# Latent attention and LoRA feed-forward on one core: low parts of the feed-forward's operands made earlier, folds moved to GpSimd, residual loaded in two transfers

## Chip, cores and metric

The kernel runs on one core of a Trainium2 chip. The metric is the device time of one execution in microseconds. The median of three runs before the change is 580.56 us. TensorE multiplies matrices into banks of PSUM; VectorE, ScalarE and GpSimd work element by element; SyncE (SP) issues the transfers. The engines run side by side and wait for each other's semaphores.

## The reference

x has 2 x 512 tokens of 512 features. Two sublayers with a layer norm before and after each:

```
x = x + layernorm(attention(layernorm(x)))     # 32 heads, latent (low-rank) queries, keys and values
x = x + layernorm(ffn(layernorm(x)))

def _qlora_linear(x, wq, A, B):                # the weight is wq repeated 4 times along its input
    return x @ tile(wq, (1, 4)).T + (x @ A.T @ B.T) * 0.5
gate = silu(_qlora_linear(x, w1q, a1, b1))     # 512 -> 1376, wq 1376 x 128, rank 2
up   = _qlora_linear(x, w3q, a3, b3)
ffn  = _qlora_linear(gate * up, w2q, a2, b2)   # 1376 -> 512, wq 512 x 344
```

Because the weight repeats 4 times, x can be folded: the four quarters of its features are added (512 to 128) and multiplied once with wq.

## The kernel before

All products are kept near float32 accuracy by splitting: an operand is written as a high part (rounded, written by ScalarE in the type fp32r) and a low part (the rest, a subtraction by VectorE or GpSimd), and `three` issues three matmuls: high x high, high x low, low x high. Much of the work of the other engines is the making of these parts.

The order of every engine is written out by hand. After the attention (until about 419 us) come three stages.

*Projection.* Eight tiles of 128 tokens. TensorE runs `project(t, hh)`: 24 matmuls for each half hh of the heads, 48 a tile. VectorE and ScalarE go through steps t = 0 to 8 beside it. In step t VectorE takes, for tile u = t-1: statistics of the product, `split_output(t, 1)` (low part of the second half of tile t, 128x1024), the first layer norm's factors, the last two of tile u-1's four `lora_dots`, the residual sum `x1 += z` (the first waits for the load of x1), statistics of the sum, `second_scale`, `split_output(t+1, 0)`, `fold_sum(u)` (a reduction of xn2 from 512 to 128 columns), the first two `lora_dots(u)` (a multiplication of xn2 with a row of a1 or a3, summed, one for each of the 4 ranks) and `lora_lo`. ScalarE makes z (layer norm of the product), xn2 (normalised sum) and the high parts. TensorE turns the folds and dots of tile t-2 in the middle of `project(t, 1)` (`turn_y`). Between the steps stand pieces for the feed-forward: in step 5 VectorE makes 3 of 12 gate/up low parts (`split_gate`), in step 6 the low part of bs_s (the LoRA-up factors, 128x1376), in step 7 the low part of the first 512 tokens' activations (xf_lo). Tile 7's second norm, fold and dots are done inside the feed-forward.

*Feed-forward.* Two halves of 512 tokens with 12 groups G each (G = 0 to 23, 128 or 88 hidden units). A group is six matmuls (gate and up), and after every second group `low_rank` adds the LoRA parts of two groups. ScalarE applies Silu, VectorE multiplies (`gu`), GpSimd adds four groups' gu into fs. Two banks' worth of lead is all TensorE has: `gate_or_up(1, G)` waits for the gu of G-3, `gate_or_up(0, G)` for its Silu; groups below 12 also wait for their `split_gate`, group 12 for the second xf_lo. `lora_down` multiplies gu with a2. In the first half VectorE makes 9 `split_gate`, tile 7's fold and dots, the b2 pair (b2 and b2_s, LoRA-down bias factors), the second xf_lo, and at group 11 wd_lo (128x1536).

*Tail.* Eight tiles of the down projection, layer norm and output.

SP issues, behind the last attention transfers: x1 (2 MB), then, once all `split_weights` are done, a13 (1 MB), w13 (1.4 MB), bs (0.7 MB); after the whole projection a2 and b2; after tile 7's dots wd.

Of the kernel before, what the change touches and what calls it, by code (L numbers as in the profile page):

```python
# [26 lines left out]
P = 128  # L27
# [58 lines left out]
def build(nc, x_d, wa_d, lnw_d, cst_d, kcs_d, sq_d, sv_d, w13_d, bs_d, a13_d, a2_d, w2_d, b2_d, out_d):  # L86
# [87 lines left out]
    w13 = pro.take("w13", [P, 2, HID])  # L174
    pr2 = Map(nc, late, late + 4 * 6 * D)
# [6 lines left out]
    ffn = Map(nc, start + 4 * P + 32 + CST_BYTES, late)  # L182
    w13_hi = ffn.take("w13_hi", [P, 2, HID], F32R)
    w13_lo = ffn.take("w13_lo", [P, 2, HID], F32R)
    bs_s = ffn.take("bs_s", [P, HID], F32R)
    xf_hi = ffn.take("xf_hi", [P, TOK], F32R)
    xf_lo = ffn.take("xf_lo", [P, TOK], F32R)
    b2 = ffn.take("b2", [P, D])
    a2 = ffn.take("a2", [P, RT, FOLD, 32])
    b2_s = ffn.take("b2_s", [P, D], F32R)  # L190
# [36 lines left out]
    def sems(phase, words):  # L227
# [13 lines left out]
    c = sems("projection", """xn2_made wv_in0 wv_in1 wv_in2 wv_copied wv_hi_made wv_split o_hi_made o_split o_used x1_in w13_in bs_in a13_in  # L241
        dve_step std1_made z_made std2_made fold_made dots_raw dots_made lt_zero y_turned xt2_moved lp_hi_made lp_split""")
# [8 lines left out]
    with block:  # L251

        @block.sync
        def _(sp):
# [82 lines left out]
            sp.dma_start(x1[:, :, :], xb.rearrange("t p d -> p t d")).then_inc(c.x1_in, 16)  # L337
            sp.wait_ge(c.wv_split, PAIRS)
            sp.dma_start(a13[:, :, :], a13_d).then_inc(c.a13_in, 16)
            sp.dma_start(w13[:, :, :], w13_d).then_inc(c.w13_in, 16)  # L340
            sp.dma_start(bs[:, :], bs_d).then_inc(c.bs_in, 16)

            sp.wait_ge(c.o_used, 2 * TB)
            sp.dma_start(a2[:, :, :, :], a2_d).then_inc(g.a2_in, 16)
            sp.dma_start(b2[:, :], b2_d).then_inc(g.b2_in, 16)
# [13 lines left out]
        def _(pool):  # L359
# [66 lines left out]

            for hf in range(2):
                for r in range(RT):
                    n = RROWS[r]
                    for k in range(1, FOLD):  # L430
                        pool.wait_ge(g.gu_made, 12 * hf + 4 * r + k + 1)
                        if (hf, r, k) != (0, 0, 1):
# [3 lines left out]
                                                gu[0:n, at(k), :], ALU.add).then_inc(g.fold_added, 1)  # L436


        @block.scalar
        def _(act):  # L440
# [80 lines left out]
            def normalise_sum(u):  # L521

                act.wait_ge(c.dve_step, 9 * u + 9)
                if u:
                    act.wait_ge(c.dots_made, u)
                nc.scalar.activation(xn2[:, :], x1[:, u, :], ACT.Identity, scale=st2[:, 11:12],
                                     bias=st2[:, 12:13]).then_inc(c.xn2_made, 1)
# [122 lines left out]
            for t in range(TB + 1):  # L650
# [21 lines left out]
                if t in (3, 4):  # L672
                    nc.scalar.activation(w13_hi[:, t - 3, :], w13[:, t - 3, :], ACT.Copy).then_inc(g.w_hi_made, 1)
                if t == 5:
                    act.wait_ge(c.o_split, 10)
                    act.wait_ge(c.bs_in, 16)
                    nc.scalar.activation(bs_s[:, :], bs[:, :], ACT.Copy, scale=cst[:, 3 * SEQ + 5:3 * SEQ + 6]).then_inc(g.bs_hi_made, 1)
# [13 lines left out]
            for hf in range(2):  # L691
                for n in range(12):
# [6 lines left out]
                    if G == 1:  # L699
                        second_deviation(TB - 1)  # L700
                        normalise_sum(TB - 1)
# [8 lines left out]
                    if G == 8:  # L710
# [8 lines left out]
                    if G == 7:  # L719
                        act.wait_ge(g.b2_in, 16)  # L720
                        nc.scalar.activation(b2_s[:, :], b2[:, :], ACT.Copy).then_inc(g.b2_hi_made, 1)
# [13 lines left out]
        def _(dve):  # L735
# [248 lines left out]
            for t in range(TB + 1):  # L984
# [5 lines left out]
                if 0 <= t - 1 < TB:  # L990
# [5 lines left out]
                    if u:  # L996
                        lora_dots(u - 1, (2, 3))
                    dve.wait_ge(c.z_made, u + 1)
                    if u == 0:
                        dve.wait_ge(c.x1_in, 16)  # L1000
                    step(nc.vector.tensor_tensor(x1[:, u, :], x1[:, u, :], zb[:, :], ALU.add), c.dve_step)
                    statistics(st2, x1[:, u, :], c.dve_step)
                    if t < TB:
# [3 lines left out]
                        fold_sum(u)  # L1007
                        lora_dots(u, (0, 1))
                if 2 <= t < TB:
                    lora_lo(t - 2)  # L1010
                if t == 5:
                    for n in range(3):
                        split_gate(n)
                if t == 6:
# [3 lines left out]
                if t == 7:  # L1018
# [18 lines left out]
            for hf in range(2):  # L1037
                for n in range(12):
# [8 lines left out]
                    if G + 3 < 12:  # L1047
                        split_gate(G + 3)
                    if G == 1:
                        second_scale(TB - 1)  # L1050
                    if G == 2:
                        fold_sum(TB - 1)
                    if G in (2, 3, 4, 5):
                        lora_dots(TB - 1, (G - 2,))
# [7 lines left out]
                    if G == 11:  # L1062
# [467 lines left out]
```

## Time and profile before

| | before |
|---|---|
| runs, us | 580.56, 580.23, 584.92 (median 580.56) |
| profiled execution | 581.56 us, of which the span of its instructions 579.7 |
| TensorE clock granted | 0.996 |
| TensorE, VectorE, ScalarE, GpSimd busy | 96%, 77%, 68%, 34% |

TensorE's busy share is near 100% almost everywhere; in the 40 slices of the span it falls a little in the feed-forward and more in the tail. Times in the trace count from the span's start. Matmuls overlap: one of 512 columns is listed with 0.39 us, but the next starts 0.23 us later. VectorE's instructions overlap by about 0.08 us in the same way.

### The profile page before, as it was taken

How to read it: one execution, taken by the hardware profiler on the slowest of the kernel's cores; microseconds unless marked ns; L12 is line 12 of the kernel's file. 1: busy time of each engine (PE TensorE's matmuls, PEld its weight loads, DVE VectorE, ACT ScalarE, POOL GpSimd, SP SyncE). 2: the span in 40 equal slices, each digit the busy share in tenths (PEclk: the TensorE clock that was granted, in tenths of full speed). 3: DMA queues.
4: the chain of work that ended last, by engine and by line, in shares of the span. 5: the costliest groups of instructions: out<-in, count | busy, mean ns of one | idle time of the engine just before them, and what ended most of it. 6: DMA issues, size and time to landing. Idle time of an engine off the chain costs nothing. (4 is left out here: it accounts for less than half of the span.)

```text
span 579.7 us, 10859 instructions
## 1 busy us (share of the span) xinstructions
PE 557.4 (96%) x3274; PEld 424.5 (73%) x3274; DVE 447.1 (77%) x1206; ACT 396.1 (68%) x1173; POOL 196.4 (34%) x204
## 2 busy tenths in 40 slices
PE   7999999999999999999999999999999999988996
PEld 6676778777787787787878878876678888645565
DVE  5877787787677777877887787888859889877467
ACT  4566778887888787878878888878733553444344
POOL 3125354344443543444344444441000000036520
PEclk8999999999999999999999999999999999999999
DMA  9911223212312222131111101006580000101003
GB/s 325 354 56 51 79 61 118 79 52 87 121 52 79 86 94 79 52 112 53 52 35 55 50 21 47 20 26 201 174 331 1 1 0 1 32 1 54 1 19 128
DMA packets 22009, 46.93 MB, mean 81 GB/s; under 512 B 2880, under 2 KB 5696, under 8 KB 21696
## 3 DMA queue, kind: packets, MB, share of 16 engines
q1 hardware_dynamic: 21952, 46.23, 23.8%
q8 instruction: 28, 0.46, 0.3%
q14 instruction: 29, 0.24, 0.1%
HBM read 39.80 MB, written 6.42 MB: 80 GB/s over the span
## 5 line engine op out<-in xcount | busy, mean ns | idle before, releaser
L766 DVE CUSTOM_DVE_ANT_0 ss<-bank,cst 128x128 f32<-128x128 f32 (+3 forms) x256 | 125.0, 489 | 72.0 <-PE bank L1130 40.9
L485 ACT ACTIVATE pt<-bank 128x128 f32<-128x128 f32 (+3 forms) x256 | 110.1, 430 | 63.2 <-PE bank L1198 62.9
L477 ACT ACTIVATE pr<-ss,small 128x128 f32<-128x128 f32 (+3 forms) x256 | 143.2, 559 | 5.8 <-DVE small L766 4.3
L373 POOL TENSOR_TENSOR qrot<-qrot,qswp 64x512 f32<-64x512 f32 x64 | 82.1, 1283 | 116.2 <-DVE qrot L758 113.7
L1198 PE MATMUL bank<-ident,pr 128*128 128x128 f32 x640 | 113.7, 275 | 1.6 <-ACT pr L477 1.5
L1198 PEld LDWEIGHTS bank<-ident,pr 128*128 128x128 f32 x640 | 78.4, 141 | 23.6 <-ACT pr L477 6.0
L380 POOL TENSOR_TENSOR qt_lo<-qrot,qt_hi 128x384 fp32r<-128x384 f32 x64 | 64.6, 1009 | 72.4 <-ACT qt_hi L467 71.3
L1128 PE MATMUL bank<-kt_hi,qt_hi 128*128 128x256 f32 (+2 forms) x192 | 80.7, 421 | 0.3 <-DVE small L766 0.3
L1210 PE MATMUL bank<-pt,kvn 128*64 128x256 f32 (+3 forms) x512 | 75.2, 434 | 0.7 <-ACT pt L485 0.7
L1210 PEld LDWEIGHTS bank<-pt,kvn 128*64 128x64 f32 x512 | 38.8, 137 | 41.0 <-issue 28.1
L1130 PE MATMUL bank<-kt_hi,qt_lo 128*128 128x256 f32 (+2 forms) x192 | 65.1, 339 | 0.0
L1129 PE MATMUL bank<-kt_lo,qt_hi 128*128 128x256 f32 (+2 forms) x192 | 64.7, 337 | 0.0
L1128 PE MATMUL bank<-wv,o_s 128*128 128x512 f32 x128 | 51.5, 402 | 1.3 <-DVE o_s L798 1.3
L1129 PE MATMUL bank<-wv,o_s 128*128 128x512 f32 x128 | 50.6, 395 | 0.0
L1130 PE MATMUL bank<-wv,o_s 128*128 128x512 f32 x128 | 50.5, 394 | 0.0
L477 ACT ACTIVATION_READ_ACCUMULATOR pr<-ss,small 128x1 f32 x256 | 49.8, 194 | 0.0
L435 POOL TENSOR_TENSOR fs<-gu 128x512 f32<-128x512 f32 (+1 forms) x6 | 8.2, 1366 | 121.7 <-DVE gu L1045 121.6
L751 DVE TENSOR_TENSOR qswp<-bank,cst 32x512 f32<-32x512 f32 x64 | 44.5, 696 | 2.0
L752 DVE TENSOR_TENSOR qswp<-bank,cst 32x512 f32<-32x512 f32 x64 | 44.2, 691 | 0.9
L758 DVE TENSOR_TENSOR qrot<-bank,cst 128x512 f32<-128x512 f32 x64 | 43.9, 686 | 0.1
L1130 PEld LDWEIGHTS bank<-kt_hi,qt_lo 128*128 128x128 f32 x192 | 36.1, 188 | 2.8
L1128 PEld LDWEIGHTS bank<-kt_hi,qt_hi 128*128 128x128 f32 x192 | 36.4, 190 | 2.0 <-DVE small L766 0.6
(184 smaller groups left out, 1103.9 us busy)
## 6 DMA issues: line engine op xcount, KB each, us to landing
rsb<-rinv_scratch SPq DMA_DIRECT2D x64, 128.0 KB, 2.9
sv<-sv SPq DMA_DIRECT2D x10, 576.0 KB, 4.7
sqa<-sq SPq DMA_DIRECT2D x16, 320.0 KB, 3.1
wv_raw<-wvo_scratch SPq DMA_DIRECT2D x8, 512.0 KB, 4.1
sve<-sv SPq DMA_DIRECT2D x6, 576.0 KB, 11.1
wvo_scratch<-vs SPq DMA_DIRECT2D x11, 256.0 KB, 2.6
xa<-x SPq DMA_DIRECT2D x8, 256.0 KB, 5.5
sqr<-sq SPq DMA_DIRECT2D x16, 128.0 KB, 2.4
```

Source lines behind the costliest of these rows:

```text
L373: nc.gpsimd.tensor_tensor(qrot[RKV:P, h, :], qrot[RKV:P, h, :], qswp[RKV:P, h, :], ALU.add)\
L380: nc.gpsimd.tensor_tensor(qt_lo[:, b, h, P:SEQ], qrot[:, h, P:SEQ], qt_hi[:, b, h, P:SEQ].bitcast(F32), ALU.subtract)\
L477: nc.scalar.activation(pr[:, k % 4, 0:n], ss[:, RING[k], 0:n], ACT.Exp, bias=negmax[:, k % 8:k % 8 + 1], scale=-1.0, accum_out=rsum[:, k:k ...
L485: nc.scalar.activation(pt[:, b, h, 0:i + 1, i * P:(i + 1) * P], bank[2 + k % 2][:, 0:(i + 1) * P].rearrange("p (j q) -> p j q", q=P), ACT. ...
L751: nc.vector.tensor_tensor(qswp[64:96, h, :], G[96:128, :], sin1[96:128, :], ALU.mult)
L752: nc.vector.tensor_tensor(qswp[96:128, h, :], G[64:96, :], sin1[64:96, :], ALU.mult)
L766: nc.vector.tensor_tensor_reduce(out=ss[:, RING[k], 0:n], in0=bank[k % 2][:, 0:n], in1=mask[:, SEQ - n:SEQ], scale=-SCALE, scalar=3.4e38, ...
L1128: nc.tensor.matmul(out, w_hi, x_hi, start=start, stop=False)
L1129: nc.tensor.matmul(out, w_hi, x_lo, start=False, stop=False)
L1130: return nc.tensor.matmul(out, w_lo, x_hi, start=False, stop=stop)
L1198: last = nc.tensor.transpose(bank[2 + k % 2][:, j * P:(j + 1) * P], pr[:, k % 4, j * P:(j + 1) * P], ident[:, :])
L1210: last = nc.tensor.matmul(bank[4][RKV * h:RKV * (h + 1), j * P:SEQ], kvn[:, QB * b + j, 0:RKV], pt[:, b, h, j, j * P:SEQ], start=(j == 0), ...
```

## The change

The low parts that VectorE makes for gate and up move into the projection: 4 in step 5, 4 in step 6, 2 at the end of step 7, and 2 remain in groups 0 and 1. The low part of bs_s moves from step 6 to step 3, the b2 pair from group 8 to step 4, the first xf_lo from step 7 to step 6; ScalarE's high parts that these need move with them. GpSimd adds up the quarters of tiles 0 to 6 in two additions (128x256, then 128x128) in place of VectorE's reduction. In the last step only one of tile 6's last two dots comes before the residual sum, the other after its statistics; tile 7's norm, fold and dots shift by a group. GpSimd makes wd_lo in three parts after folds of the feed-forward, and ScalarE's wd_hi moves from group 8 to group 12. x1 comes in two transfers, tiles 0 and 1 first, the rest behind a13; bs goes before w13, and b2 and a2 are loaded during the projection. Tiles b2, b2_s and bs_s get places that are free earlier. New semaphores are not shown.

```diff
--- before.py
+++ after.py
@@ -172,6 +172,7 @@
...
     w13 = pro.take("w13", [P, 2, HID])
+    half = pro.take("half", [P, 2, P])
     pr2 = Map(nc, late, late + 4 * 6 * D)
@@ -180,14 +181,14 @@
...
     ffn = Map(nc, start + 4 * P + 32 + CST_BYTES, late)
+    bs_s = ffn.take("bs_s", [P, HID], F32R)
+    b2_s = ffn.take("b2_s", [P, D], F32R)
+    b2 = ffn.take("b2", [P, D])
     w13_hi = ffn.take("w13_hi", [P, 2, HID], F32R)
     w13_lo = ffn.take("w13_lo", [P, 2, HID], F32R)
-    bs_s = ffn.take("bs_s", [P, HID], F32R)
     xf_hi = ffn.take("xf_hi", [P, TOK], F32R)
     xf_lo = ffn.take("xf_lo", [P, TOK], F32R)
-    b2 = ffn.take("b2", [P, D])
     a2 = ffn.take("a2", [P, RT, FOLD, 32])
-    b2_s = ffn.take("b2_s", [P, D], F32R)
     l2 = ffn.take("l2", [P, 2, SEQ], F32R)
@@ -334,15 +335,16 @@
...
             sp.wait_ge(a.o_made, 2 * PAIRS)
-            sp.dma_start(x1[:, :, :], xb.rearrange("t p d -> p t d")).then_inc(c.x1_in, 16)
+            sp.dma_start(x1[:, 0:2, :], xb[0:2].rearrange("t p d -> p t d")).then_inc(c.x1_first, 16)
             sp.wait_ge(c.wv_split, PAIRS)
             sp.dma_start(a13[:, :, :], a13_d).then_inc(c.a13_in, 16)
+            sp.dma_start(x1[:, 2:TB, :], xb[2:TB].rearrange("t p d -> p t d")).then_inc(c.x1_in, 16)
+            sp.dma_start(bs[:, :], bs_d).then_inc(c.bs_in, 16)
             sp.dma_start(w13[:, :, :], w13_d).then_inc(c.w13_in, 16)
-            sp.dma_start(bs[:, :], bs_d).then_inc(c.bs_in, 16)
-
-            sp.wait_ge(c.o_used, 2 * TB)
+            sp.wait_ge(c.o_split, 4)
+            sp.dma_start(b2[:, :], b2_d).then_inc(g.b2_in, 16)
+            sp.wait_ge(c.o_split, 12)
             sp.dma_start(a2[:, :, :, :], a2_d).then_inc(g.a2_in, 16)
-            sp.dma_start(b2[:, :], b2_d).then_inc(g.b2_in, 16)
             sp.wait_ge(c.dots_made, TB)
@@ -424,6 +426,15 @@
...
+            for u in range(TB - 1):
+                pool.wait_ge(c.xn2_made, u + 1)
+                nc.gpsimd.tensor_tensor(half[:, :, :], xn2[:, 0:2 * P].rearrange("p (c n) -> p c n", c=2),
+                                        xn2[:, 2 * P:D].rearrange("p (c n) -> p c n", c=2), ALU.add).then_inc(c.half_made, 1)
+                pool.wait_ge(c.half_made, u + 1)
+                if u >= 2:
+                    pool.wait_ge(c.y_turned, u - 1)
+                nc.gpsimd.tensor_tensor(fold[:, u % 2, :], half[:, 0, :], half[:, 1, :], ALU.add).then_inc(c.fold_made, 1)
+
             for hf in range(2):
@@ -434,6 +445,11 @@
...
                                                 gu[0:n, at(k), :], ALU.add).then_inc(g.fold_added, 1)
+                    if (hf, r) in ((0, 2), (1, 0), (1, 1)):
+                        q = (r + 1) % RT
+                        pool.wait_ge(g.wd_hi_made, 1)
+                        nc.gpsimd.tensor_tensor(wd_lo[:, q, :], wd[:, q, :], wd_hi[:, q, :].bitcast(F32), ALU.subtract)\
+                          .then_inc(g.wd_split, 1)
@@ -523,6 +539,7 @@
...
                     act.wait_ge(c.dots_made, u)
+                    act.wait_ge(c.fold_made, u)
                 nc.scalar.activation(xn2[:, :], x1[:, u, :], ACT.Identity, scale=st2[:, 11:12],
@@ -671,10 +688,15 @@
...
                     nc.scalar.activation(w13_hi[:, t - 3, :], w13[:, t - 3, :], ACT.Copy).then_inc(g.w_hi_made, 1)
+                if t == 2:
+                    act.wait_ge(c.o_split, 2)
+                    act.wait_ge(c.bs_in, 16)
+                    nc.scalar.activation(bs_s[:, :], bs[:, :], ACT.Copy, scale=cst[:, 3 * SEQ + 5:3 * SEQ + 6]).then_inc(g.bs_hi_made, 1)
+                if t == 3:
+                    act.wait_ge(g.b2_in, 16)
+                    nc.scalar.activation(b2_s[:, :], b2[:, :], ACT.Copy).then_inc(g.b2_hi_made, 1)
                 if t == 5:
                     act.wait_ge(c.o_split, 10)
-                    act.wait_ge(c.bs_in, 16)
-                    nc.scalar.activation(bs_s[:, :], bs[:, :], ACT.Copy, scale=cst[:, 3 * SEQ + 5:3 * SEQ + 6]).then_inc(g.bs_hi_made, 1)
                     act.wait_ge(c.xt2_moved, QB)
@@ -698,6 +720,7 @@
...
                         second_deviation(TB - 1)
+                    if G == 2:
                         normalise_sum(TB - 1)
@@ -707,7 +730,7 @@
...
                         nc.scalar.activation(xf_hi[:, SEQ:TOK], xft[:, SEQ:TOK], ACT.Copy).then_inc(g.xf_hi_made, 1)
-                    if G == 8:
+                    if G == 12:
                         act.wait_ge(g.wd_in, 16)
@@ -716,9 +739,6 @@
...
                         lora_down_hi(0)
-                    if G == 7:
-                        act.wait_ge(g.b2_in, 16)
-                        nc.scalar.activation(b2_s[:, :], b2[:, :], ACT.Copy).then_inc(g.b2_hi_made, 1)
             down_hi(1, RT - 1)
@@ -994,28 +1014,42 @@
...
                     if u:
-                        lora_dots(u - 1, (2, 3))
+                        lora_dots(u - 1, (2, 3) if t < TB else (2,))
                     dve.wait_ge(c.z_made, u + 1)
-                    if u == 0:
-                        dve.wait_ge(c.x1_in, 16)
+                    if u in (0, 2):
+                        dve.wait_ge(c.x1_in if u else c.x1_first, 16)
                     step(nc.vector.tensor_tensor(x1[:, u, :], x1[:, u, :], zb[:, :], ALU.add), c.dve_step)
...
                             split_output(t + 1, 0)
-                        fold_sum(u)
+                        if t == 7:
+                            split_gate(8)
+                            split_gate(9)
+                        dve.wait_ge(c.xn2_made, u + 1)
                         lora_dots(u, (0, 1))
+                    else:
+                        lora_dots(u - 1, (3,))
                 if 2 <= t < TB:
                     lora_lo(t - 2)
-                if t == 5:
-                    for n in range(3):
+                if t in (5, 6):
+                    for n in range(4 * t - 20, 4 * t - 16):
                         split_gate(n)
-                if t == 6:
+                if t == 4:
+
+                    dve.wait_ge(g.b2_hi_made, 1)
+                    nc.vector.scalar_tensor_tensor(b2[:, :], b2[:, :], cst[:, 3 * SEQ + 3:3 * SEQ + 4],
+                                                   b2_s[:, :].bitcast(F32), ALU.mult, ALU.subtract)\
+                      .then_inc(g.b2_lo_made, 1)
+                    dve.wait_ge(g.b2_lo_made, 1)
+                    nc.vector.tensor_scalar(b2_s[:, :], b2[:, :], cst[:, 3 * SEQ + 4:3 * SEQ + 5], None, ALU.mult)\
+                      .then_inc(g.b2_split, 1)
+                if t == 3:
                     dve.wait_ge(g.bs_hi_made, 1)
...
                                                    ALU.mult, ALU.add).then_inc(g.bs_split, 1)
-                if t == 7:
+                if t == 6:
                     dve.wait_ge(g.xf_hi_made, 1)
@@ -1044,14 +1078,14 @@
...
                                             ALU.mult).then_inc(g.gu_made, 1)
-                    if G + 3 < 12:
-                        split_gate(G + 3)
+                    if G < 2:
+                        split_gate(G + 10)
                     if G == 1:
                         second_scale(TB - 1)
-                    if G == 2:
+                    if G == 3:
                         fold_sum(TB - 1)
-                    if G in (2, 3, 4, 5):
-                        lora_dots(TB - 1, (G - 2,))
+                    if G in (3, 4, 5):
+                        lora_dots(TB - 1, {3: (0,), 4: (1, 2), 5: (3,)}[G])
                     if G == 4:
@@ -1059,19 +1093,6 @@
...
                                                 ALU.subtract).then_inc(g.xf_split, 1)
-                    if G == 11:
-                        dve.wait_ge(g.wd_hi_made, 1)
-                        nc.vector.tensor_tensor(wd_lo[:, :, :], wd[:, :, :], wd_hi[:, :, :].bitcast(F32), ALU.subtract)\
-                          .then_inc(g.wd_split, 1)
-                    if G == 8:
-
-                        dve.wait_ge(g.b2_hi_made, 1)
-                        nc.vector.scalar_tensor_tensor(b2[:, :], b2[:, :], cst[:, 3 * SEQ + 3:3 * SEQ + 4],
-                                                       b2_s[:, :].bitcast(F32), ALU.mult, ALU.subtract)\
-                          .then_inc(g.b2_lo_made, 1)
-                        dve.wait_ge(g.b2_lo_made, 1)
-                        nc.vector.tensor_scalar(b2_s[:, :], b2[:, :], cst[:, 3 * SEQ + 4:3 * SEQ + 5], None, ALU.mult)\
-                          .then_inc(g.b2_split, 1)
                     if n == 8:
@@ -1432,7 +1453,7 @@
...
                         lora_down(0, RT - 1)
-            pe.wait_ge(g.wd_split, 1)
+            pe.wait_ge(g.wd_split, RT)
             pe.wait_ge(g.b2_split, 1)
...
```

## Rows read from the trace of the kernel before

**Rows 1.** Waits of TensorE from 417 us on: us in total, times, longest.

```profile
PE bank L1128 <- DVE w_lo L976: 3.6, 4, 1.3
```

**Rows 2.** Timeline of TensorE: start us, us, engine, line, operation, idle before and releaser.

```profile
430.20 0.40 PE L1130 MATMUL bank<-wv,o_s 128*128 128x512 f32 x1
431.89 0.50 PE L1128 MATMUL bank<-wv,o_s 128*128 128x512 f32 x1 [1.30 <-DVE o_s L798]
...
500.20 0.39 PE L1130 MATMUL bank<-wv,o_s 128*128 128x512 f32 x1
501.19 0.50 PE L1128 MATMUL bank<-xf_hi,w_hi 128*128 128x512 f32 x1 [0.59 <-DVE xf_lo L1020]
...
530.03 0.50 PE L1128 MATMUL bank<-xf_hi,w_hi 128*128 128x512 f32 x1 [1.58 <-DVE xf_lo L1060]
...
533.44 1.06 PE L1401 MATMUL bank<-gu,a 88*32 88x512 f32 x8
...
553.36 0.50 PE L1128 MATMUL bank<-wd_hi,fs_hi 128*128 128x512 f32 x1
```

**Rows 3.** Timeline of VectorE in the projection and at its end.

```profile
427.59 0.69 DVE L1001 TENSOR_TENSOR x<-x,zb 128x512 f32<-128x512 f32 x1 [5.28 <-DMA x<-x]
...
478.30 0.70 DVE L934 BATCH_NORM_STATS2 st<-bank 128x6 f32<-128x512 f32 x1
...
479.25 1.22 DVE L798 TENSOR_TENSOR o_s<-ot,o_s 128x1024 fp32r<-128x1024 f32 x1
...
490.53 0.70 DVE L934 BATCH_NORM_STATS2 st<-bank 128x6 f32<-128x512 f32 x1
...
501.05 0.69 DVE L934 BATCH_NORM_STATS2 st<-bank 128x6 f32<-128x512 f32 x1
...
502.83 0.69 DVE L960 CUSTOM_DVE_ANT_0 dot<-xn,a 128x512 f32<-128x512 f32 x1
...
506.00 0.69 DVE L1045 TENSOR_TENSOR gu<-bank,sg 128x512 f32<-128x512 f32 x1
```

**Rows 4.** DMA issues from 400 us on: KB each, median us to landing.

```profile
wv_raw<-wvo_scratch SPq DMA_DIRECT2D x5, 512.0 KB, 3.8
x<-x SPq DMA_DIRECT2D x1, 2048.0 KB, 11.4
```

**Rows 5.** Groups by shape, VectorE, from 417 us on: busy us, mean ns.

```profile
L949 DVE TENSOR_REDUCE fold<-xn 128x128 f32<-128x512 f32 x8 | 8.6, 1075 | 0.9 <-ACT xn L526 0.9
...
L976 DVE TENSOR_TENSOR w_lo<-w,w_hi 128x256 fp32r<-128x256 f32 x8 | 3.2, 417 | 0.0
...
L1016 DVE SCALAR_TENSOR_TENSOR bs_s<-bs,cst,bs_s 128x1376 fp32r<-128x1376 f32 x1 | 1.6, 1646 | 0.0
...
L1069 DVE SCALAR_TENSOR_TENSOR b<-b,cst,b_s 128x512 f32<-128x512 f32 x1 | 0.7, 741 | 0.0
```

**Rows 6.** Groups by shape, GpSimd, whole execution.

```profile
L380 POOL TENSOR_TENSOR qt_lo<-qrot,qt_hi 128x384 fp32r<-128x384 f32 x64 | 64.6, 1009 | 72.4 <-ACT qt_hi L467 71.3
...
L386 POOL TENSOR_TENSOR w_lo<-sqr,w_hi 128x128 fp32r<-128x128 f32 x16 | 7.3, 458 | 9.3 <-ACT w L454 9.3
```

**Rows 7.** Timeline of all engines, where GpSimd and VectorE meet.

```profile
514.54 1.39 POOL L435 TENSOR_TENSOR fs<-fs,gu 128x512 f32<-128x512 f32 x1 [1.25 <-DVE gu L1045]
514.71 1.77 DVE L960 CUSTOM_DVE_ANT_0 dot<-xn,a 128x512 f32<-128x512 f32 x1
...
530.65 3.32 POOL L435 TENSOR_TENSOR fs<-fs,gu 88x512 f32<-88x512 f32 x1 [1.23 <-DVE gu L1045]
...
531.10 1.74 DVE L1064 TENSOR_TENSOR wd_lo<-wd,wd_hi 128x1536 fp32r<-128x1536 f32 x1
```

**Rows 8.** Timeline of ScalarE at the end of the projection.

```profile
503.63 1.28 ACT L697 ACT_TABLE_LOAD   x1
```

**Rows 9.** Timeline of GpSimd late in the second half.

```profile
547.18 2.70 POOL L435 TENSOR_TENSOR fs<-fs,gu 128x512 f32<-128x512 f32 x2 [2.51 <-DVE gu L1045]
551.70 1.28 POOL L435 TENSOR_TENSOR fs<-gu 88x512 f32<-88x512 f32 x1 [1.82 <-DVE gu L1045]
```

More of the change, by code:

```diff
@@ L240, in build @@
         wvo_made wvo_moved wvo_out""")
-    c = sems("projection", """xn2_made wv_in0 wv_in1 wv_in2 wv_copied wv_hi_made wv_split o_hi_made o_split o_used x1_in w13_in bs_in a13_in
-        dve_step std1_made z_made std2_made fold_made dots_raw dots_made lt_zero y_turned xt2_moved lp_hi_made lp_split""")
+    c = sems("projection", """xn2_made wv_in0 wv_in1 wv_in2 wv_copied wv_hi_made wv_split o_hi_made o_split o_used x1_first x1_in w13_in bs_in a13_in
+        dve_step std1_made z_made std2_made half_made fold_made dots_raw dots_made lt_zero y_turned xt2_moved lp_hi_made lp_split""")
     g = sems("forward", """wd_in b2_in a2_in w_hi_made w_split xf_hi_made xf_split bs_hi_made bs_split bs_fixed wd_hi_made wd_split
```

## Prediction

> **What bounds the kernel now.** Read first the waits of TensorE in the part behind attention, then its timeline at the places where a wait ends, then what VectorE did just before. TensorE is the bound: its products of the output projection follow each other every 0.233 us, and from the first one after the wait at 431.89 to the last at 500.20 six token tiles take 500.43 - 431.89 = 68.5 us, 11.42 us a tile, without a gap [rows 2]. So only what makes TensorE stand still can be won. There are three such places.
> - Projection, tile 2: from 430.20 to 431.89 is 1.69 us where 0.23 would do, so 1.46 us are lost [rows 2]. The splitting of the output stood behind the residual sum, which waited 5.28 us for the 2 MB residual [rows 3].
> - Into the feed-forward: 500.20 to 501.19, 0.76 us over the pace; it waits for the low part of the activations [rows 2].
> - First half of the feed-forward, groups 0 to 11: 530.03 - 501.19 = 28.84 us. The second half takes 553.36 - 530.03 = 23.33 us with no wait and with three LoRA-down steps of 1.0 us (first at 533.44), the first half has two and two turnings of tiles (0.33 together, an estimate from their short products). Undisturbed it would be 23.33 - 1.0 + 0.33 = 22.7 us, so 6.1 us are lost [rows 2]. The waits name the gate and up low parts (3.6 us in 4 waits) [rows 1] and the second low part of the activations (1.58) [rows 2]; the rest, 6.1 - 5.2 over five waits, is the slower restart after each, some 0.2 us a time.
>
> Together 8.3 us. Behind 553.36 lies a tail of 26 us (the down projection and the last layer norm), whose order the change leaves as it is.
>
> **The change, part by part.** *Residual in two transfers.* The first two tiles (512 KB) go alone. A 512 KB load landed in 3.8 us, the 2 MB one in 11.4 [rows 4]; issued at 416.0 the first lands at about 420, and VectorE asks for it at 427.59 - 5.28 = 422.3 [rows 3]. So the wait of 5.28 us becomes none, VectorE runs ahead of TensorE by about 3 us at tile 2, and the 1.46 us go. Of the loads behind it a13 is needed first: with the first tiles it makes 1.5 MB, about 8 us at the rate of the 2 MB, so it lands near 425, ahead of the first dots (427). If it came no earlier than now, the 1.46 stays.
>
> *Folds to GpSimd.* VectorE's fold costs 1.08 us by its row, 1.0 of own time since starts overlap by 0.08 [rows 5]; seven of eight leave it. GpSimd does each as 128x256 and 128x128. It took 458 ns for 128x128 and 1009 for 128x384 [rows 6]; halfway between is 0.73, so 0.73 + 0.46 = 1.2 us a tile. Nobody waits for the result itself: it is turned more than half a tile later. What matters is VectorE beside it. The dot at 514.71 took 1.77 us [rows 7] where the one at 502.83 took 0.69 [rows 3]: GpSimd's op had begun at 514.54 and ran to 515.93, and the dot did its work only then. The other way round, GpSimd's op at 530.65 took 3.32 us, where one of its size takes 1.28 [rows 9], and VectorE's 1536-column op at 531.10 ran undisturbed in it [rows 7]. In the changed kernel both start from ScalarE's high part of the next tile: ScalarE then needs 0.8 us for xn2, GpSimd's input, VectorE 1.2 for the split [rows 3]. So GpSimd comes some 0.4 us before VectorE is through, and the two dots follow. Lower bound of the cost to VectorE is 0, upper 0.73 + 0.46 = 1.2 us a tile. I take 1.2, by the nearest row: at 514.54 GpSimd also came while VectorE was in a two-input op, and VectorE's next op was the one held.
>
> The Trainium skill (SBUF — State Buffer, "Who interferes with whom") says that a VectorE instruction with two SBUF inputs and a GpSimd instruction that reads SBUF exclude each other, the first to start holding the port to its end, and that a reduction never contends: the fold is such a reduction, so the rule speaks against moving it. By it VectorE gains nothing; without it, 1.0 us a tile. The pair at 514.54 agrees, the pair at 530.65 does not: there the later one went first.
>
> *Low parts earlier.* Now tile step 6 of VectorE takes 490.53 - 478.30 = 12.23 us [rows 3], of which 1.57 is the LoRA-up low part [rows 5]: 10.66 for the bare step, with the fold. Without the fold 9.66; with GpSimd's 1.2, 10.86. TensorE's tile is 11.42. Added: step 3 the LoRA-up low part 1.57; step 4 the b2 pair, 0.74 and a shorter one, 1.07 together as an estimate; step 5 four gate/up parts at 0.34 (0.42 less overlap) = 1.36; step 6 four more and the activations' low part 0.6 = 1.96 [rows 5]. VectorE's lag behind TensorE: step 3 10.86 + 1.57 - 11.42 = 1.0; step 4 1.5; step 5 2.3; step 6 3.7. The split of a tile's second half ends 2.2 us into a step (479.25 + 1.22 - 478.30) and is needed 5.6 in [rows 3]: slack 3.4. That of the next tile's first half ends at about 8.2 and is needed at 11.4: slack 3.2. So only step 7 stalls TensorE, by 0.3 and a restart, 0.5. Step 7 itself now takes 501.05 - 490.53 = 10.52 [rows 3]; less fold 1.0, less activations 0.6, with gate parts 8 and 9 inside its 0.9 us of idle [rows 5]: 8.9, plus 1.2 = 10.1. Lag at the last tile: 3.7 + 10.1 - 11.9 = 1.9 us.
>
> *Feed-forward, first half.* The 0.76 us go: the activations' low part is long made. With 10 of 12 gate parts made, the next thing late is VectorE's group 0. Now statistics start at 501.05, z ends at 503.63 where the Silu table load begins [rows 8], and group 0's product is at 506.00 [rows 3]. In the new order z (2.6), sum 0.65, statistics 0.9, one dot 0.65, copies 0.35, product 0.65 end 5.8 to 5.9 us after the statistics start. TensorE asks for it at its fourth group, 5.5 us in. With no lag that is a stall of 0.6 + 0.2 restart; a second follows at group 7, because in group 3 the fold of tile 7 (1.0) and a dot (0.6, up to 1.0 beside GpSimd) come before the product of group 4: 0.5 + 0.2. With 1.9 us of lag z too is late, and the two waits together take 2.1 us more. Last, the second activations' low part is ready about 22 us after the start, TensorE needs it at 24: no wait.
>
> *Down low parts on GpSimd.* They leave VectorE 1.7 us at group 11, where it isn't late. GpSimd gets three ops of 1.3 us. The last follows the folds that end now at 549.88 and so ends near 551.2; the next fold starts at 551.70, after 1.82 us of idle, and TensorE needs the weights at 553.36 [rows 2, 9]. So it costs nothing while 0.5 us of that idle is left, and each us beyond would push the last folds, and with them the tail, by as much. ScalarE's high part of wd, moved to group 12, delays Silu 13 by 1.5 us; TensorE wants it two groups later. SP's waits are on events that pass well before the loads are used.
>
> **Sum.** 8.3 - 0.8 - 0.7 (stalls in the first half) - 2.1 (lag) - 0.5 (step 7) = 4.2 to 4.3 us less. The profiled execution took 581.56 (span 579.7 and 1.9 around it) and comes to 577.3; against the median of 580.56, 1.0 below it, I forecast 576.3.
>
> **Rivals.** (a) GpSimd doesn't hold up the dots. Then steps take 9.66 + additions, at most 11.6, no lag is left, and only the two stalls (1.5) remain: 6.8 us less, 573.7. For it: the undisturbed op at 531.10 [rows 7], and that VectorE's ops follow back to back. Against: the dot at 514.71. (b) Gain mostly gone, 577.5 to 580.5: the dot cost is nearer 1.6 a tile, or the first transfer saves nothing. (c) Slower: GpSimd's small ops hold VectorE for more than their length, as the 3.32 us op shows that one can stretch. At x us a tile, five steps lag by 5(9.66 + x - 11.42) + 5.96, of which 3.2 is slack; TensorE's new stalls outweigh the old 8.3 from x = 1.8 on. At 2.4 it is 3.4 us slower, 584.0. Against: both single rows give 1.2 for the pair.
>
> **Chances.** Forecast 0.48, (a) 0.30, (b) 0.14, (c) 0.08. The range, 572.8 to 579.5, takes in (a) with 1 us below, and most of (b); the floor with all stalls gone is 572.2. One per cent, 5.8 us, is about what a measurement of this kernel can tell from no change. Faster by over that (below 574.8): (a) and a little of the forecast, 0.35. Slower by over it (above 586.4): 0.03. The rest, 0.62, lies between.
>
> **What would show it.** Right: no wait of TensorE at tile 2, the residual sum without a wait; TensorE's waits in the first half name the product gu, not w_lo or xf_lo; dots of 1.2 to 1.8 us in the projection next to GpSimd's folds; statistics of the last tile about 2 us behind TensorE. Dots all at 0.69 would mean (a). Waits of TensorE for o_s at every tile would mean (c). Wrong altogether: a wait for the down weights or for the first a13 load.

## The result, and the profile after

| | before | after |
|---|---|---|
| median on the same chips, us | 582.58 (580.23 to 584.92) | 574.99 (574.45 to 576.57) |
| profiled execution, us (span) | 581.56 (579.7) | 574.45 (572.7) |

The ratio is 0.9871 with a 95% interval of 0.9838 to 0.9905, so 1.3% or 7.5 us less. A second timing of the same kernel on another occasion gave 575.13 against 583.68, ratio 0.9848 (0.9828 to 0.9868). Three executions on a third occasion, far off all others (694.2 and 1110.73 us of the kernel before, 790.31 of a changed one), are in no median or ratio of this document. The two profiled executions lie 7.1 us apart. Where these went is read in the order of the prediction. First the waits of TensorE after the change, from 410 us on (us in total, times, longest); the names answer to [rows 1]:

```profile
PE bank L1149 <- ACT z L750: 0.6, 1, 0.6
PE bank L1149 <- DVE gu L1079: 0.4, 1, 0.4
PE bank L1149 <- ACT sg L719: 0.3, 1, 0.3
PE bank L1149 <- DVE xf_lo L1094: 0.2, 1, 0.2
```

The waits for w_lo (3.6 us), for o_s (1.3) and for the first xf_lo (0.6) are gone, and the second xf_lo costs 0.2 where it cost 1.6. Apart from the tail's z, 0.9 us of waits are left. TensorE's timeline at the points of [rows 2]:

```profile
497.99 0.39 PE L1151 MATMUL bank<-wv,o_s 128*128 128x512 f32 x1
498.22 0.40 PE L1149 MATMUL bank<-xf_hi,w_hi 128*128 128x512 f32 x1
...
503.59 0.47 PE L1149 MATMUL bank<-xf_hi,w_hi 128*128 128x512 f32 x1 [0.27 <-ACT sg L719]
...
504.87 0.50 PE L1149 MATMUL bank<-xf_hi,w_hi 128*128 128x512 f32 x1 [0.35 <-DVE gu L1079]
...
522.99 0.50 PE L1149 MATMUL bank<-xf_hi,w_hi 128*128 128x512 f32 x1 [0.17 <-DVE xf_lo L1094]
...
546.35 0.50 PE L1149 MATMUL bank<-wd_hi,fs_hi 128*128 128x512 f32 x1
```

The feed-forward follows the projection without a gap (0.23 us from 497.99 to 498.22, before 0.99: 0.76 us won). Its first half takes 522.99 - 498.22 = 24.77 us, before 28.84 (4.1 won). The second takes 23.36, before 23.33. The rest is ahead of it. The last group of products of the attention starts at 409.56 before and at 408.99 after, which is no part of the change; from there to the last product of the projection it is 90.64 and 89.00 us (1.6 won). Together 6.5 us by the change and 0.6 from ahead of it.

Now VectorE and GpSimd, all engines but TensorE, at the first tile:

```profile
425.64 1.23 DVE L818 TENSOR_TENSOR o_s<-ot,o_s 128x1024 fp32r<-128x1024 f32 x1 [0.54 <-ACT o_s L525]
426.32 1.14 POOL L431 TENSOR_TENSOR half<-xn 128x256 f32<-128x256 f32 x1 [31.32 <-ACT xn L543]
426.78 1.23 DVE L980 CUSTOM_DVE_ANT_0 dot<-xn,a 128x512 f32<-128x512 f32 x1
427.54 0.79 POOL L436 TENSOR_TENSOR fold<-half 128x128 f32<-128x128 f32 x1
...
427.95 0.94 DVE L980 CUSTOM_DVE_ANT_0 dot<-xn,a 128x512 f32<-128x512 f32 x1
```

This is a chain of alternating holds. GpSimd's first addition is ready at 426.32, in the middle of VectorE's split, and ends only at 427.46. VectorE's dot, next in its queue, takes 1.23 us in place of 0.69. GpSimd's second addition waits for that dot (0.79, alone 0.46), and holds the second dot (0.94). Tiles 1 to 5 repeat these lengths within 0.02 us; at tile 6, where no split stands ahead, the first dot is free (0.69) and the second is held (1.22). VectorE loses 0.54 + 0.25 = 0.8 us a tile, against the 1.0 us of the reduction that it no longer makes. And VectorE's statistics, which mark how far it is behind TensorE [rows 3]:

```profile
487.02 1.06 ACT L525 ACTIVATE o_s<-ot 128x1024 fp32r<-128x1024 f32 x1 [1.82 <-PE bank L1151]
...
489.57 0.68 DVE L954 BATCH_NORM_STATS2 st<-bank 128x6 f32<-128x512 f32 x1
...
498.98 0.68 DVE L954 BATCH_NORM_STATS2 st<-bank 128x6 f32<-128x512 f32 x1
```

The last product of tile 6 ends at about 487.0 (ScalarE, which waits for it, starts at 487.02), that of tile 7 at 497.99 + 0.39 = 498.4. So VectorE is 2.5 us behind in step 7 and 0.6 at the last tile.

The last of the waits, 0.2 us for the second xf_lo, has a hold in it too, outside the folds of the tiles:

```profile
521.09 1.30 POOL L446 TENSOR_TENSOR fs<-gu 88x512 f32<-88x512 f32 x1 [1.55 <-DVE gu L1079]
521.19 1.75 DVE L1094 TENSOR_TENSOR xf_lo<-xft,xf_hi 128x512 fp32r<-128x512 f32 x1
```

This low part takes 1.75 us, where the first xf_lo takes 0.68 (at 488.96): GpSimd's addition of gu into fs began 0.1 us before it. It ends 24.7 us after the start of the feed-forward.

### The profile page after: what moved, and what is told of

Its sections match the earlier page's. It is cut to its first block and busy times, and to the rows that moved or that the text cites. A ratio compares the mean times of both kernels' runs of the same rounds, so it can differ in the third digit from the quotient of the medians.

```text
span 572.7 us, 10879 instructions
## 1 busy us (share of the span) xinstructions
PE 556.4 (97%) x3274; PEld 423.2 (74%) x3274; DVE 444.4 (78%) x1198; ACT 396.2 (69%) x1173; POOL 212.3 (37%) x221
## 5 line engine op out<-in xcount | busy, mean ns | idle before, releaser
L431 POOL TENSOR_TENSOR half<-xn 128x256 f32<-128x256 f32 x7 | 8.1, 1156 | 89.9 <-ACT xn L543 79.9
```

## Experiments

The first column below is the median of the timed runs with the ratio to the kernel before on the same chip (95% interval). The rows come from three occasions; before's median was 583.68 us for the four rows from "changed, again" to "gate parts late", 583.33 for residual only, three halves, down parts on VectorE and product first, 582.69 for the last three. The interval of a ratio is 1.1 to 1.6 us wide to each side, so a difference below about 1 us between two rows rests on the traces. The other columns are read from TensorE's timeline of the profiled execution: from the last attention product to the last of the projection, the first half of the feed-forward, the second half.

| kernel | median us | ratio | projection | first | second |
|---|---|---|---|---|---|
| before, first look | 580.56 | | 90.6 | 28.8 | 23.3 |
| before, another look | 584.06 (one) | | 89.8 | 29.9 | 26.1 |
| changed, again | 575.13 | 0.9848 (0.9828 to 0.9868) | 89.0 | 24.8 | 23.4 |
| fold on VectorE | 575.91 | 0.9864 (0.9843 to 0.9885) | 89.2 | 25.7 | 23.4 |
| folds in the gap | 573.84 | 0.9833 (0.9812 to 0.9853) | 88.9 | 24.2 | 23.4 |
| gate parts late | 577.10 | 0.9880 (0.9861 to 0.9899) | 89.1 | 26.3 | 23.4 |
| residual only | 580.34 | 0.9961 (0.9940 to 0.9982) | 89.0 | 30.4 | 25.9 |
| three halves | 578.56 | 0.9916 (0.9898 to 0.9935) | 91.2 | 25.3 | 23.4 |
| down parts on VectorE | 577.73 | 0.9898 (0.9879 to 0.9918) | 89.1 | 26.7 | 24.8 |
| gap, product first | 574.86 | 0.9862 (0.9836 to 0.9888) | 89.0 | 24.2 | 23.4 |
| down parts moved, in before | 580.06 | 0.9956 (0.9937 to 0.9975) | 90.4 | 27.8 | 23.3 |
| gap, once more | 574.13 | 0.9869 (0.9841 to 0.9897) | 89.0 | 24.2 | 23.4 |
| gap, tile 7's fold on GpSimd | 573.89 | 0.9861 (0.9834 to 0.9887) | 89.0 | 24.3 | 23.4 |

**The changed kernel again.** No edit.

> The changed kernel once more, as the measure for the three beside it. Its span was 7.0 us shorter than that of the kernel before, of which 0.6 lie ahead of the projection and so are not the change's. Expected again: 6.4 to 7.5 us less than before.

It was 8.5 us below before, more than the 6.4 to 7.5 expected. Its trace repeats the first within 0.1 us stage by stage.

**Fold on VectorE.** The GpSimd loop over the tiles goes, and in each step:

```diff
-                        dve.wait_ge(c.xn2_made, u + 1)
+                        fold_sum(u)
                         lora_dots(u, (0, 1))
```

> The changed kernel with the folds of tiles 0 to 6 back on VectorE. Theory 1 (the port): GpSimd's fold held up VectorE's dots by 0.54 and 0.25 us a tile in the changed kernel, 0.8 of the 1.0 us that it saves, so the fold's move is worth 0.2 us a tile; VectorE's step 6 ends 0.2 x 4 = 0.8 us later, its statistics of the last tile come about 1 us later, and the time is 0.5 to 1.0 us above the changed kernel's, 6 us below before. Theory 2 (the fold's move pays for the rest): without it VectorE is 1.0 us a tile later, from step 3 on by 4 to 5 us, TensorE waits for o_s at tile 7, and the time is 3 us or more above the changed kernel's.

It took 0.8 us more than the changed kernel; the first half is 0.9 longer, where TensorE waits 1.0 us for ScalarE's z of the last tile. So the move of the fold alone is worth about 0.8 us, within the 0.5 to 1.0 of theory 1 and far from theory 2.

**Folds in the gap.** One more wait for GpSimd, which puts its two additions beside the statistics of the next tile's sum:

```diff
                 pool.wait_ge(c.xn2_made, u + 1)
+                pool.wait_ge(c.dve_step, 9 * (u + 1) + 5)
```

> The changed kernel with one wait more for GpSimd: it folds tile u after the residual sum of tile u+1, when VectorE does statistics, a one-input instruction, and waits for ScalarE. Theory 1 (two-input instructions exclude GpSimd's): all dots of the projection take 0.69 us, GpSimd's additions 0.73 and 0.46 instead of 1.14 and 0.79, VectorE's lag at the last tile falls from 0.6 us to 0.2, and the time by 0.3 to 0.5 us. Theory 2 (GpSimd's additions are as slow as in the changed kernel for another reason, such as their access pattern): they stay at 1.1 and 0.8 us here too.

The groups by shape from 417 to 503 us, mean ns after the busy time:

```profile
L981 DVE CUSTOM_DVE_ANT_0 dot<-xn,a 128x512 f32<-128x512 f32 x28 | 18.6, 699 | 0.5 <-ACT xn L544 0.2
...
L432 POOL TENSOR_TENSOR half<-xn 128x256 f32<-128x256 f32 x7 | 5.1, 734 | 99.1 <-DVE x L1022 99.1
...
L437 POOL TENSOR_TENSOR fold<-half 128x128 f32<-128x128 f32 x7 | 3.2, 458 | 0.5
```

Dots and additions have their undisturbed lengths (but for one dot at 502.75, 0.99 us, which an addition overlaps); the 0.73 and 0.46 us of the forecast are exact. Since only the moment changed, theory 2 is out: the longer times of the changed kernel come from the additions' meeting with the split and the dots, which read two SBUF inputs. The Trainium skill (SBUF — State Buffer, "Who interferes with whom") states that a VectorE instruction with two SBUF inputs contends with a GpSimd instruction that reads SBUF, and that one with at most one such input does not. The trace agrees: beside statistics, which have one input, the additions take 0.73 us and the statistics 0.69. VectorE's lag goes with the hold:

```profile
487.51 0.69 DVE L955 BATCH_NORM_STATS2 st<-bank 128x6 f32<-128x512 f32 x1
...
498.47 0.70 DVE L955 BATCH_NORM_STATS2 st<-bank 128x6 f32<-128x512 f32 x1 [1.86 <-PE bank L1152]
```

Read as above, it is 0.4 us behind in step 7 instead of 2.5, and at the last tile VectorE waits for the product. The median is 1.3 us below the changed kernel's of the same occasion, and 573.84 and 574.13 in two timings against 574.99 and 575.13; in the traces it is 0.6 us, in the first half, a little over the 0.3 to 0.5 expected. It is the version to keep, by a margin that the ratios alone (0.9833 and 0.9869 against 0.9871 and 0.9848) would not show.

**Gate parts late.** The twelve gate and up low parts at their old places in an otherwise changed kernel:

```diff
-                if t in (5, 6):
-                    for n in range(4 * t - 20, 4 * t - 16):
+                if t == 5:
+                    for n in range(3):
                         split_gate(n)
...
-                    if G < 2:
-                        split_gate(G + 10)
+                    if G + 3 < 12:
+                        split_gate(G + 3)
```

(the two of step 7 go as well)

> The changed kernel with the gate and up low parts where they were: three in step 5, the others after each group's product. Theory 1 (TensorE waited for them because each stands behind a product, a fold or a dot on VectorE): the waits for w_lo return, 2.5 to 4 us, and the time is 3 to 5 us above the changed kernel's. Theory 2 (VectorE is as late in the first half as ever, only with the waits under another name, gu for w_lo): under 1.5 us above the changed kernel's, and before's 6.1 us went with the other pieces moved (b2 pair, down low parts, LoRA-up low part).

2.0 us more than the changed kernel (1.5 in the trace's first half), between the theories. The wait for w_lo is back with 2.1 us, not with the 3.6 of before:

```profile
PE bank L1146 <- DVE w_lo L996: 2.1, 3, 1.5
```

So 1.5 of the 3.6 us went with the other moves; which of them took it away isn't shown.

**Residual only.** In the kernel before, x1 in two transfers with a13 between them, and the two waits for them in VectorE.

> The kernel before with the residual in two transfers and nothing else. Theory 1 (the forecast's term): the wait for the residual goes from 5.3 us to none, TensorE's wait at tile 2 goes, and the time falls by 1.5 us. Theory 2 (VectorE's lag is the bound from there on, and the wait comes back later): under 0.5 us.

The projection took 89.0 us, 1.6 less than in the first look at before, and TensorE's wait for o_s is gone: theory 1's term. In the other look at before, below, that wait was 0.4 us and not 1.3, so there the term is only 0.8. The median fell by 3.0 us, twice what theory 1 expected, and the ratio gives 2.3; the rest isn't explained. This very trace is no shorter than before's (span 581.3). Its second half takes 25.9 us instead of 23.3, and TensorE's clock tells why, in the next look.

**The kernel before, another look.**

> The kernel before once more, for one look. Its first profiled execution took 581.6 us, 1.8 below the median of later runs, and had no stretch at half clock ahead of the tail. Theory 1: in most executions TensorE's clock falls after the wait ahead of group 12, as in the two kernels with longer waits there, and the half behind it takes up to 2.5 us more; this look then shows about 583 to 585 us with the second half at 24 us or more. Theory 2: the spread comes from ahead of the projection; then the second half takes 23.3 us again and the start of the projection differs.

584.06 us. ScalarE, then GpSimd and VectorE, then TensorE ahead of group 12:

```profile
525.27 1.49 ACT L712 ACTIVATE wd_hi<-wd 128x1536 fp32r<-128x1536 f32 x1 [1.70 <-DMA wd<-w]
526.67 0.57 ACT L697 ACTIVATE sg<-bank 88x512 f32<-88x512 f32 x1
...
527.55 0.63 ACT L709 ACTIVATE xf_hi<-xft 128x512 fp32r<-128x512 f32 x1
```

```profile
528.04 1.26 POOL L435 TENSOR_TENSOR fs<-gu 88x512 f32<-88x512 f32 x1 [4.67 <-DVE gu L1045]
528.21 1.65 DVE L1060 TENSOR_TENSOR xf_lo<-xft,xf_hi 128x512 fp32r<-128x512 f32 x1
```

```profile
529.91 0.80 PE L1128 MATMUL bank<-xf_hi,w_hi 128*128 128x512 f32 x1 [2.60 <-DVE xf_lo L1060]
530.50 0.63 PE L1129 MATMUL bank<-xf_lo,w_hi 128*128 128x512 f32 x1
530.93 0.63 PE L1130 MATMUL bank<-xf_hi,w_lo 128*128 128x512 f32 x1
```

and the stretches around it (stretch, length, busy time and instructions of each engine, granted clock, DMA share, GB/s):

```profile
523.00:530.00 7.00, 4.40 (x25) 2.07 (x24) 5.41 (x9) 4.97 (x9) 1.64 (x2) 0.94 0.06 21
530.00:532.00 2.00, 2.00 (x5) 1.61 (x6) 2.00 (x3) 0.00 (x0) 1.47 (x1) 0.50 0.00 0
532.00:535.00 3.00, 3.00 (x8) 2.10 (x7) 0.72 (x1) 0.00 (x0) 2.86 (x2) 0.50 0.00 0
535.00:540.00 5.00, 5.00 (x25) 2.63 (x24) 1.89 (x3) 1.60 (x3) 1.94 (x2) 0.90 0.00 0
```

In group 8 ScalarE waits 1.7 us for the load of wd, makes the 1.5 us high part, then Silu 9, then the activations' high part. VectorE's xf_lo starts that much later, 28.2 us after the start of the feed-forward and not 27.1 as in the first look, and takes 1.65 us instead of 0.68 because GpSimd's addition holds it. TensorE stands still for 2.6 us. Its clock falls to 0.50, the lower of its two levels (1.2 GHz), while it still stands: 0.94 over the first 7 us of the table is 0.8 us at the lower level, ahead of 530. It stays there until about 536 (0.90 over the last 5 us), with products 0.43 us apart instead of 0.23. The second half takes 26.1 us: 2.7 lost on top of the wait.

In the first look xf_lo was held too (1.71 us), but ScalarE waited only 0.52 us for wd and was in time: there the wait was 1.58 us, 1.03 of it the hold, and no stretch at the lower clock followed. What differed was the load: wd landed 4.1 us after its issue in the first look, 5.3 us in this one and 5.7 in residual only, where TensorE waited 3.08 us.

Executions of the kernel before range from 580 to 585 us. For 39 of the timed ones the mean granted clock is known: the 12 with 0.996 or more took 581.5 us on average, the 15 with 0.993 or less 584.1, and this traced one has 0.993, the first look 0.996. So theory 1 is shown for this execution and fits the spread of the others, though a mean clock doesn't say where it fell.

**Down parts on VectorE.** The changed kernel with wd_lo and wd_hi where they were: one VectorE instruction at group 11, ScalarE's high part at group 8.

> The changed kernel with the down low parts back on VectorE at group 11, as one instruction, and ScalarE's high part back at group 8. Theory 1 (VectorE isn't late there and GpSimd has room): within 0.3 us of the changed kernel. Theory 2: VectorE's 1.7 us instruction holds up GpSimd's folds, so that the last fold of the half is later and something behind it waits: 0.5 us or more above.

Neither theory's cause: 2.6 us more, and not through GpSimd's folds. ScalarE and TensorE:

```profile
520.23 1.49 ACT L730 ACTIVATE wd_hi<-wd 128x1536 fp32r<-128x1536 f32 x1 [1.19 <-DMA wd<-w]
```

```profile
524.86 0.80 PE L1148 MATMUL bank<-xf_hi,w_hi 128*128 128x512 f32 x1 [2.09 <-DVE xf_lo L1089]
```

The chain of the look before, in the changed kernel. xf_lo is held by GpSimd in both (1.64 us here, 1.75 in the changed kernel), but starts 25.0 us after the start of the feed-forward instead of 23.0. These 2.0 us are ScalarE's. TensorE waits 2.1 us, then runs for 3 us at the lower clock; the first half is 1.9 and the second 1.5 us longer.

**Down parts moved, in the kernel before.**

```diff
-                    if G == 8:
+                    if G == 12:
                         act.wait_ge(g.wd_in, 16)
                         nc.scalar.activation(wd_hi[:, :, :], wd[:, :, :], ACT.Copy).then_inc(g.wd_hi_made, 1)
```

and wd_lo on GpSimd as in the change.

> The kernel before with the down low parts on GpSimd and ScalarE's high part in group 12, nothing else. Theory 1 (what the move frees is not VectorE but ScalarE: in group 8 the high part waits for the load of wd and takes 1.5 us, ahead of Silu 9 and of the activations' high part, so the low part comes late and TensorE waits ahead of group 12, after which its clock is at the lower level for some us): TensorE's wait of 1.6 us for xf_lo goes, no stretch at half clock follows, and the time falls by 1.5 to 4 us. Theory 2 (the forecast's: the move is worth nothing, VectorE isn't late there): under 0.5 us.

2.6 us less, as theory 1 expected. The wait ahead of group 12 is 0.5 us, and no stretch at half clock follows:

```profile
PE bank L1129 <- DVE xf_lo L1065: 0.5, 1, 0.5
```

Seen from both sides, added alone and taken back alone, the move is worth 2.6 us. But this trace doesn't show ScalarE as the cause:

```profile
527.12 1.93 POOL L435 TENSOR_TENSOR fs<-gu 88x512 f32<-88x512 f32 x1 [3.63 <-DVE gu L1050]
527.22 0.68 DVE L1065 TENSOR_TENSOR xf_lo<-xft,xf_hi 128x512 fp32r<-128x512 f32 x1
```

xf_lo starts 27.1 us after the start of the feed-forward, exactly as in the first look. It is 1.03 us shorter, since here VectorE went first and GpSimd's addition took 1.93 us, and that is the whole of the difference to the first look's 1.58. Against the look at 584.06, 1.1 us of the wait went with ScalarE's delay and 1.0 with the hold. Why this order fell the other way is open: in all 13 other traces xf_lo is the one held, 1.64 to 1.75 us. How the 2.6 us divide between ScalarE, the hold and the clock isn't separated.

**Three halves.** GpSimd repeats its first addition twice for each tile, with the same values:

```diff
+                for again in (1, 2):
+                    pool.wait_ge(c.half_made, 3 * u + again)
+                    nc.gpsimd.tensor_tensor(half[:, :, :], xn2[:, 0:2 * P].rearrange("p (c n) -> p c n", c=2),
+                                            xn2[:, 2 * P:D].rearrange("p (c n) -> p c n", c=2), ALU.add).then_inc(c.half_made, 1)
```

> The changed kernel with GpSimd's first addition made three times over for each tile (the same values, so the output stands). Theory 1 (each GpSimd addition can hold up one two-input instruction of VectorE): VectorE is held by 0.5 us at each dot and, in steps 3, 5 and 6, at the part behind the dots; about 0.3 us a tile more in steps 2 and 4, 0.8 in the others, so its lag at the last tile rises from 0.6 to some 2.5 us, TensorE's stalls by about 2 to 3 us; still faster than before. Rival (c), that from 1.8 us a tile on the change makes the kernel slower: 2 us or more above before.

3.4 us more than the changed kernel, somewhat over the 2 to 3 expected (2.6 in the trace, from the last attention product to the end of the feed-forward); now TensorE waits in the projection too:

```profile
PE bank L1153 <- DVE o_s L822: 1.3, 1, 1.3
...
PE bank L1153 <- ACT zb L679: 0.6, 1, 0.6
```

In step 6 the two dots take 1.22 us each and the four gate parts 1.96 in place of 1.42, so VectorE is held for 1.6 us there. This is the mechanism of rival (c) at twice the real size, near the 1.8 us a tile from which it was to cost more than the change gives, and the kernel is still 4.8 us faster than before.

**Product first, and tile 7's fold on GpSimd.** On top of the folds in the gap, tile 6's last dot goes behind group 0's product; then tile 7's fold too goes to GpSimd, between its first two additions of fs:

```diff
                     else:
-                        lora_dots(u - 1, (3,))
...
+                    if G == 0:
+                        lora_dots(TB - 2, (3,))
```

> The folds in the gap as in the run before, and tile 6's last dot after group 0's product, not before it. The product of group 0 is then ready 0.6 us earlier than in the changed kernel. Theory 1 (TensorE's two waits at group 3, 0.27 and 0.35 us, are for Silu 0 and for this product): the second goes, and with the earlier statistics the first too; the time is 0.7 to 1.2 us below the changed kernel's. Theory 2 (the next thing is late at once, the Silu behind two table loads): under 0.4 us below, and a wait for sg of group 2 or 3 appears.

> The folds in the gap once more, as the measure for the next: 573.5 to 574.5 us.

> Folds in the gap, group 0's product ahead of tile 6's last dot, and tile 7's fold on GpSimd between its first two additions of fs. The product-first run had its wait moved from group 3 to group 7, where VectorE's fold (1.0 us) and a dot (1.3) stand ahead of group 4's product. Theory 1: with the fold gone that product is 1 us earlier, the wait at group 7 goes, tile 7's dots and the second low part of the activations are ready earlier too, and the time is 0.5 to 1.0 us below that of the folds in the gap. Theory 2 (Silu and its table loads are the next bound): under 0.3 us.

Neither gave anything over the folds in the gap, against the 0.5 to 1.0 us of theory 1 for the last: 574.86 and 573.89 against 573.84 and 574.13, first half 24.2, 24.3 and 24.2. With the product first, the wait at group 3 is gone but one of 0.3 us appears ahead of group 7, for gu and not for Silu's output, as theory 2 had it. With the fold gone too, no wait for gu is left:

```profile
PE bank L1157 <- ACT z L758: 0.6, 1, 0.6
PE bank L1390 <- issue: 0.6, 1, 0.6
PE bank L1157 <- DVE xf_lo L1102: 0.2, 1, 0.2
```

Both end at group 12 with the same 0.2 us for xf_lo. What holds TensorE at the turning of a tile (issue 0.6) in the last one was not followed further.

## Why the prediction was right, and where it was not

The forecast, 576.3 us from a median of 580.56, was 4.3 less; it came to 7.5 less, and the time of 574.99 lies within the range. That the time is only 1.3 us off is in part luck: the gain was forecast 3.2 us too small, and the base, the median of three runs, was 2.0 us below the 582.58 of the comparison. Direction, places and the bound (TensorE's waits) were right; the size was short by almost half.

- *Residual.* Forecast 1.46 us, measured 1.6 against the first look (projection 90.6 to 89.0, and alone in the kernel before), 0.8 against the other. Right for the execution it was read from.
- *Into the feed-forward.* Forecast 0.76, measured 0.76. Right.
- *GpSimd's hold on VectorE.* The mechanism was right, each addition holding one dot. The size was 0.8 us a tile, not 1.2: each addition held its dot about 0.2 us less than its own length (0.54 of 0.73, 0.25 of 0.46). Why isn't shown. The step was to take the upper bound, the additions' whole length, where the row at 514.54 already had a dot held by 1.1 us beside an addition of 1.39. The lag that came from it was 2.5 us at step 7, forecast 3.7, and 0.6 at the last tile, forecast 1.9. So the stall of step 7 (0.5) did not come, and the 2.1 us charged to the lag were mostly absent: taking out the hold altogether, by the folds in the gap, brought the lag at step 7 to 0.4 us and won 0.6 us in the trace. By the first half's length the stalls in it are 24.77 - 22.7 = 2.1 us, forecast 0.8 + 0.7 + 2.1 = 3.6.
- *Down low parts.* The step "They leave VectorE 1.7 us at group 11, where it isn't late", with ScalarE's move priced only by what it delays in group 12, is the one that failed. It looked at what the moved piece leaves on VectorE and at what it meets in its new place, not at who stood behind it in its old one, on ScalarE. That was the second activations' high part, and ahead of it a wait for a load. The wait of 1.6 us for xf_lo had been counted among those won, without its cause: had ScalarE's piece stayed, a wait of 2.1 us would have stood there (down parts on VectorE). The sum of 4.3 didn't suffer by it, since it credited the wait's end all the same.
- *Second xf_lo.* "Ready about 22 us after the start, TensorE needs it at 24": it was ready at 24.7, for a wait of 0.2. The forecast didn't see that GpSimd's addition of gu into fs holds it for 1.07 us, as it had in the kernel before (1.03 of the 1.58 us). That so little came of it is luck.
- *Clock.* Not in the forecast. Its median was based on an execution in which the wait ahead of group 12 had no consequence; in others it is followed by the lower clock and costs 2.7 us more. This is the likeliest source of the 1 us by which before's median in the later runs (582.58 and more) is above the profiled execution, and so of the gap between 7.5 measured and 6.5 found in the traces. By the executions' mean clocks it is frequent; traced it is in one execution of before.
- *Gate parts.* Counted within the 6.1 us; alone they are worth 2.0.

Rival (a), at 573.7, is as near to the result as the forecast, but its condition didn't hold: the dots were held up, as it denied. Rival (c) needed twice the real load even to make TensorE wait in the projection, and was then still far from its point. Its limit of 1.8 us a tile doesn't come out of its own formula either: at 1.8 that gives 3.0 us of new stalls in the projection, with the 1.5 and 2.1 of the feed-forward 6.6, less than the 8.3.

## What to carry to other kernels

When a piece of work moves, ask for every instruction of it, the high part on the other engine included, who was queued behind it in the old place and what it waited for there; a wait for a load in the middle of an in-order queue delays all that follows. Look at the length of the late piece as well as at its start: here it took 1.7 us where its twin took 0.7, since another engine held it. GpSimd beside VectorE costs little if its two-input instructions are put beside VectorE's one-input ones; a single wait did that here. When executions of a kernel spread by 1%, look at a second profile before taking the first as the base.

## What the runs showed of the hardware that was not expected

TensorE's granted clock fell to 0.50 (1.2 GHz) during waits of 2.09, 2.60 and 3.08 us ahead of group 12 (down parts on VectorE, the other look at before, residual only), and stayed there for 3 to 6 us of full work behind them; with 1.58 us in the first look at before, and with 0.5, it did not fall. Such a wait so cost 1.5, 2.7 and 2.6 us more behind it.

In the changed kernel a GpSimd addition that comes during a two-input instruction of VectorE goes next, ahead of the VectorE instruction already queued (all seven tiles). The opposite order stays unexplained: it is in [rows 7], at the same place of the other look at before, residual only and down parts on VectorE, and at xf_lo in down parts moved, where GpSimd began 0.10 us earlier, just as in the first look and the changed kernel, in which it went first.

The same load of wd (768 KB) landed 3.9 to 4.3 us after its issue in nine of the 14 traces and 5.0 to 5.8 us in the other five. Why isn't shown.
